# Adding the five weighed branches of a gated mix on VectorE instead of on TensorE

## The reference

```python
gate_in = jnp.concatenate([hidden_states, _stats(short), _stats(long_), _stats(wide), _stats(delta_out), _stats(v)], -1)
hdn = jax.nn.gelu(gate_in @ g1_w.T + g1_b, approximate=False)
logits = (hdn @ g2_w.T + g2_b).reshape(b, Ll, H, 5)
p = jax.nn.softmax(logits, -1)
o = w_ctx[..., 0:1] * short + w_ctx[..., 1:2] * long_ + w_ctx[..., 2:3] * wide + w_ctx[..., 3:4] * delta_out + w_val * v
o = o * jax.lax.rsqrt(jnp.mean(o * o, -1, keepdims=True) + 1e-05) * onorm_w
return o.reshape(b, Ll, HID) @ o_w.T
```

## Time and profile before

| what | value |
|---|---|
| time, median of 3 runs | 745.3 us (739.52 to 745.67) |
| the profiled execution | 743.56 us, of which the span is 741.8 us |
| busy over the span | PE 83%, PEld 60%, DVE 59%, ACT 38%, POOL 15% |
| stage 3 | about 350 to 480 us |

### The profile page before, as it was taken

How to read it: one execution, slowest core, us unless ns; L and a number is a source line. 1 busy time by engine, 2 the same in 40 slices (tenths; PEclk the granted TensorE clock), 3 DMA queues, 4 the chain that set the end, 5 groups by cost and what they waited for, 6 DMA issues and landing times. The chain is left out here.

```text
span 741.8 us, 17132 instructions
## 1 busy us (share of the span) xinstructions
PE 619.3 (83%) x7532; PEld 443.7 (60%) x7544; DVE 440.9 (59%) x878; ACT 283.9 (38%) x518; POOL 111.5 (15%) x93
## 2 busy tenths in 40 slices
PE   4668879999998999686999957499999784998984
PEld 2365466777767777675344545377787672655643
DVE  2942567848766785748176764203358593667764
ACT  2665534433443443214343532123232325554431
POOL 0001340250061025000101221162100010000000
PEclk9968999999999999978899997589999987999988
DMA  6500520330151031003200106030000000000001
GB/s 173 188 2 3 175 83 4 117 114 4 31 166 38 4 115 59 4 3 92 81 0 1 57 29 246 3 111 1 1 0 1 0 1 0 1 1 29 29 0 58
DMA packets 26537, 37.52 MB, mean 51 GB/s; under 512 B 4641, under 2 KB 13602, under 8 KB 26463
## 3 DMA queue, kind: packets, MB, share of 16 engines
q1 hardware_dynamic: 26463, 36.42, 15.2%
HBM read 34.31 MB, written 2.10 MB: 49 GB/s over the span
## 5 line engine op out<-in xcount | busy, mean ns | idle before, releaser
L295 DVE SCALAR_TENSOR_TENSOR arena<-bank,conv_w,arena 128x511 f32<-128x511 f32 (+2 forms) x72 | 53.1, 746 | 30.3 <-ACT arena L1056 14.7
L1428 POOL COPY arena<-v_win 128x256 f32<-128x256 f32 x32 | 21.1, 688 | 194.8 <-PE bank L718 194.7
L2071 ACT COPY arena<-bank 128x512 f32<-128x512 f32 x40 | 23.5, 586 | 63.4 <-PE bank L1956 38.5
L1956 PE MATMUL bank<-v_win,arena 128*128 128x256 f32 x192 | 45.7, 386 | 0.0
L2420 PE MATMUL bank<-v_win,arena 128*128 128x256 bf16 x288 | 36.5, 279 | 7.9 <-DVE arena L2507 6.9
L718 PE MATMUL bank<-arena 128*32 128x128 f32 x512 | 35.7, 409 | 8.2 <-ACT arena L1067 7.0
L1112 ACT COPY arena<-bank 128x512 f32<-128x512 f32 x40 | 21.6, 589 | 51.6 <-PE bank L840 51.6
L1956 PEld LDWEIGHTS bank<-v_win,arena 128*128 128x128 f32 x192 | 35.3, 190 | 8.6 <-issue 4.4
L1072 ACT COPY arena<-bank 128x256 f32<-128x256 f32 x32 | 19.3, 604 | 54.0 <-PE bank L731 54.0
L2410 PE MATMUL bank<-arena,v_win 128*128 128x512 bf16 x134 | 36.2, 400 | 3.7 <-DVE arena L2478 3.2
L2420 PEld LDWEIGHTS bank<-v_win,arena 128*128 128x128 bf16 x288 | 28.4, 100 | 16.6 <-DVE arena L2507 7.9
(11 more groups left out here) (274 smaller groups left out, 1389.8 us busy)
## 6 DMA issues: line engine op xcount, KB each, us to landing
arena<-in_toep_w SPq DMA_DIRECT2D x32, 256.0 KB, 2.9
arena<-in_toep_l SPq DMA_DIRECT2D x32, 256.0 KB, 3.6
arena<-in_xT SPq DMA_DIRECT2D x12, 512.0 KB, 4.7
arena<-in_x SPq DMA_DIRECT2D x4, 512.0 KB, 4.9
arena<-in_ctx SPq DMA_DIRECT2D x4, 512.0 KB, 3.9
out<-arena SPq DMA_DIRECT2D x4, 512.0 KB, 2.9
qkv_w<-in_qkv_wT SPq DMA_DIRECT2D x1, 768.0 KB, 5.3
v_win<-in_w_gateT SPq DMA_DIRECT2D x1, 768.0 KB, 6.7
```

The source lines that it names most:

```text
L295: return nc.vector.scalar_tensor_tensor(out=acc[:, j:L], in0=src[:, 0:L - j], scalar=conv_w[:, m, CONV_K - 1 - j:CONV_K - j], in1=acc[:, j:L],
L1956: i = mm(oo, src[:, k, f * P:(f + 1) * P], w[:, k, :], start=(k == 0), stop=(k == KT - 1 and f > 0))
L2071: nc.scalar.copy(dst(i), bank[n % RING].rearrange("p (t c) -> p t c", c=dst(i).shape[-1]))\
```

## The change

VectorE makes the whole sum. `weigh_rest(b)` has three more additions behind its old last one: `ps` plus `pwl` into `pd` over all 1024 columns, and then `pv` onto `pd` in two halves of 512 columns. The first waits for its direct predecessor in the queue, and the first half for the first. `mix_squares` and `head_norm` read `pd` in VectorE's memory (the view `o_half`) instead of banks 6 and 7. The twelve identity products of a batch go, with their waits, and on TensorE `statistics(b+2)` now comes between `logits(b+1)` and `turn_logits(b+1)`. No DMA is changed.

```diff
-                def mix(b, t):
-                    if t == 0:
-                        pe.wait_ge(s3["p_wl"].sem, s3["p_wl"].at(b, 3))
-                        pe.wait_ge(s3["p_v"].sem, s3["p_v"].at(b, 1))
-                        pe.wait_ge(s3["p_sd"].sem, s3["p_sd"].at(b, 3))
...
-                    mm(o, ident[:], A3[b % 2]["pv"][:, t, :], start=True, stop=False)
-                    mm(o, ident[:], A3[b % 2]["ps"][:, t, :], start=False, stop=False)
-                    i = mm(o, ident[:], A3[b % 2]["pwl"][:, 0, t, :], start=False, stop=True)
...
                     if b < B - 1:
                         logits(b + 1)
-                    mix(b, 0)
+                    if b < B - 2:
+                        statistics(b + 2)
                     if b < B - 1:
                         turn_logits(b + 1)
-                    mix(b, 1)
-                    if b < B - 2:
-                        statistics(b + 2)
-                    mix(b, 2)
-                    mix(b, 3)
...
-                        act.wait_ge(s3["mix_mm"].sem, s3["mix_mm"].at(b, i2 + 1))
-                        a(A3[b % 2]["sq_b"][:, i2 * 2 * D:(i2 + 1) * 2 * D], mix_bank(i2)[:], ACT.Square)\
+                        act.wait_ge(s3["o_sum"].sem, s3["o_sum"].at(b, i2 + 2))
+                        a(A3[b % 2]["sq_b"][:, i2 * 2 * D:(i2 + 1) * 2 * D], o_half(b, i2), ACT.Square)\
...
                     v.tensor_tensor(A3[u]["ps"], A3[u]["ps"], A3[u]["pd"], ALU.add).then_inc(s3["p_sd"].sem, 1)
+                    dve.wait_ge(s3["p_wl"].sem, s3["p_wl"].at(b, 3))
+                    dve.wait_ge(s3["p_sd"].sem, s3["p_sd"].at(b, 3))
+                    v.tensor_tensor(A3[u]["pd"], A3[u]["ps"], A3[u]["pwl"][:, 0, :, :], ALU.add).then_inc(s3["o_sum"].sem, 1)
+                    dve.wait_ge(s3["p_v"].sem, s3["p_v"].at(b, 1))
+                    dve.wait_ge(s3["o_sum"].sem, s3["o_sum"].at(b, 1))
+                    for i2 in range(2):
+                        t = slice(2 * i2, 2 * i2 + 2)
+                        v.tensor_tensor(A3[u]["pd"][:, t, :], A3[u]["pd"][:, t, :], A3[u]["pv"][:, t, :], ALU.add)\
+                            .then_inc(s3["o_sum"].sem, 1)
...
-                                        mix_bank(i2)[:].rearrange("p (g c) -> p g c", c=DK),
+                                        o_half(b, i2).rearrange("p (g c) -> p g c", c=DK),
```

More of the change, by code:

```diff
@@ L576, in layer @@
             "last_root": 0, "st_turned": 1, "st_out": 1, "hdn_mm": 4, "gelu": 4, "lg_mm": 1, "lg_rows": 1, "lg_rows_out": 1,
-            "lg_pre": 4, "lg_exp": 1, "lg_post": 5, "p_wl": 3, "p_v": 1, "p_sd": 3, "mix_mm": 2, "mix_sq": 2, "mix_ss": 4,
+            "lg_pre": 4, "lg_exp": 1, "lg_post": 5, "p_wl": 3, "p_v": 1, "p_sd": 3, "o_sum": 3, "mix_sq": 2, "mix_ss": 4,
             "r_head": 2, "o_turned": 2, "o_norm": 2, "oT_out": 2, "y_mm": 2, "res": 2, "ln_st": 9, "ln_rs": 1, "nm_out": 1,
@@ L1488, in layer, with o_half @@
         ST_BANK, LG_BANK = 0, 4
-        hid_bank, mix_bank, turn3_bank, y_bank = (lambda m: bank[2 + m % 2]), (lambda i2: bank[6 + i2]), (lambda k: bank[(1, 5)[k]]), (lambda i2: bank[i2])
+        def o_half(b, i2):
+            return A3[b % 2]["pd"][:, 2 * i2:2 * i2 + 2, :].rearrange("p t c -> p (t c)")
+        hid_bank, turn3_bank, y_bank = (lambda m: bank[2 + m % 2]), (lambda k: bank[(1, 5)[k]]), (lambda i2: bank[i2])
         with nc.Block() as block:
@@ L1553, in turn_logits @@
                     nc.tensor.transpose(bank[LG_BANK][:, P:2 * P], A3[b % 2]["lgr"], ident[:]).then_inc(s3["lg_mm"].sem, 1)
-                def mix(b, t):
-                    if t == 0:
-                        pe.wait_ge(s3["p_wl"].sem, s3["p_wl"].at(b, 3))
-                        pe.wait_ge(s3["p_v"].sem, s3["p_v"].at(b, 1))
-                        pe.wait_ge(s3["p_sd"].sem, s3["p_sd"].at(b, 3))
-                        if b:
-                            pe.wait_ge(s3["o_norm"].sem, s3["o_norm"].at(b - 1, 2))
-                    o = mix_bank(t // 2)[:, (t % 2) * D:(t % 2 + 1) * D]
-                    mm(o, ident[:], A3[b % 2]["pv"][:, t, :], start=True, stop=False)
-                    mm(o, ident[:], A3[b % 2]["ps"][:, t, :], start=False, stop=False)
-                    i = mm(o, ident[:], A3[b % 2]["pwl"][:, 0, t, :], start=False, stop=True)
-                    if t % 2:
-                        i.then_inc(s3["mix_mm"].sem, 1)
                 def turn_o(b):
```

## The result

The changed kernel takes 756.8 us (median of 4 runs, 752.69 to 758.24) against 743.94 us (median of 4, 739.52 to 745.67) for the kernel before: 1.0173 times as long, 95% interval 1.0109 to 1.0237. It is slower, the profiled execution by 14.5 us (758.09 against 743.56). Whoever reads only the medians learns little of the change, since the stages ahead of stage 3 bring up to 15 us of their own: in the thirteen profiles of this document stage 3 starts between 342.6 and 358.0 us, with the same work ahead of it. The trace divides the sum.

The account below looks back on a forecast made before the run. VectorE and TensorE were taken as balanced to 0.25 us in rounds 0 and 1. Profiled 743.6 plus 5.4 for the queues plus 5.8 for TensorE's clock gave 754.8 us, range 748.5 to 759.5.

Parts of the forecast that it names:

- The balance of 0.25 us: Rounds 0 and 1: VectorE would release turn_o only 0.25 us before TensorE is ready, so relieving TensorE gives back only that.
- a = 2.60: VectorE's weigh_rest: the three new additions lengthen it by 2.60 us a batch, with bounds 2.4 and 2.7.
- +3.04 and +2.35 by the queues: Delay from VectorE's additions without clock effects: +3.04 us in round 0, +2.35 in round 1, +5.4 in all.
- The clock, 2.9 a round: TensorE's turn_o and project in rounds 0 and 1 run at low clock after idling: 2.9 us each, 5.8 for two.
- the plain case: Both projections of rounds 0 and 1 at low clock, no slow hidden: 5.4 + 5.8 = 11.2 us, giving 754.8.
- Rounds 2 and 3 at nothing: weigh_rest(3)'s 2.60 us more stays under VectorE's 3.29 us idleness before residual(2), with 0.7 to spare: 0 added.
- The port at nothing: head_norm reading two SBUF operands beside GpSimd's power adds nothing; the lockout rival gave 756.6, chance 0.04.
- A clock that stays up (749.0): Rival: TensorE's clock stays full in rounds 0 and 1, leaving only 743.6 + 5.4 = 749.0 us; chance 0.09.
- TensorE as the pace (733.2): Rival: TensorE sets the pace and loses 5.2 us in each of two rounds, 733.2 us; chance of faster 0.05.
- No effect (743.6): Rival: the additions lie in unseen waits of VectorE and count in no round, 743.6 us; chance 0.04.
- The allowance of 1.7 for the median: Part of the range's upper end: 1.7 us because the median of runs lay above the profiled run.
- the two rows of the prediction, 2.22 and 3.10 us: TensorE idle stretches in the old profile: 2.22 us left the clock at 1.00; in one of 3.10 it fell.

Follow-up runs that it names:

- The queue order alone: Kernel before with TensorE's statistics and turn_logits put ahead of all twelve identity products, the sum staying on TensorE: stage 3 131.4 us, ratio 0.9974.
- spare products: Changed kernel with unread identity products in TensorE's idle stretches of rounds 0, 1: ratio 1.0104; kernel before with them in rounds 2, 3: 0.994, then 0.9928.
- the run without additions: Changed kernel without its three VectorE additions, the sum left out: stage 3 134.9 us, ratio 1.0054 to the kernel before.
- the halfway kernel: Kernel before with one more full VectorE addition, eight identity products a batch, changed TensorE queue order, unread products in rounds 2 and 3: 741.65 us, ratio 0.9948.

## Why the prediction was right

The forecast was 754.8 us, the range 748.5 to 759.5, slower by over 1% at 0.71. The measured 756.8 is 2.0 above it, and the mechanism is the one that was named: VectorE becomes the later engine in rounds 0 and 1, and TensorE's clock falls in the pauses. Stage 3 alone became 10.5 us longer against a sum of 11.2, but three errors are in that: the queues cost 0.6 more than the sum, rounds 2 and 3 cost 0.4 more (within their spread), and the clock 1.6 less. That they nearly cancel is luck.

- **The balance of 0.25 us.** Held. The queue order alone moved stage 3 by 0.4 and its first stretch by -0.4, and the additions put beside the old sum reproduced the whole loss.
- **a = 2.60.** Measured 390.10 - 386.24 = 3.86 from L1763 to the next step, less the old 1.14: 2.72 a batch, just above the upper bound of 2.7. The dependent steps start 0.10 after their predecessor's end (386.24 + 1.22 = 387.46, then 387.56), where I took 0.04 from instructions of 80 columns.
- **+3.04 and +2.35 by the queues.** With the clock kept up, 60.0 - 56.4 = 3.6 and 26.7 - 24.3 = 2.4. The queue sum was 5.4 and is 6.0: a counts three times in it, 0.36, and the 0.2 that is left stands ahead of the mix, in code that is the same (`logits(1)` starts 31.3 us after the stage's start with spare products and 31.0 in the kernel before).
- **The clock, 2.9 a round.** Overestimated: 2.6 and 1.5, 4.2 in place of 5.8. The term that was mis-sized is `hidden` behind its own pause, which I left out of the plain case and gave at most 1.5. In round 0 the clock had fallen in the pause before `hidden(2)`'s third product (391.98, 0.50 until 398). From there to the end `hidden(2)` took 13.2 us in place of 10.0, so the gap ahead of `turn_o(0)` was 3.25 and not 6.3. In round 1 `hidden(3)` began later than I had it (the wait for its input) and took 13.5 in place of 11.8, behind a pause of 4.15. The late start is not what closed the gap: with the load put earlier, the pause moved to the third product, and the end of `hidden(3)` stayed. The gap ahead of `turn_o(1)` was 1.57 and not 4.4, `turn_o(1)` ran at full clock with 1.09, and the clock fell only behind it, inside the pause for ScalarE: half the price, 5.25 for `project(1)` in place of 6.1. Of the signs that I had named, "idle for 4 to 6 us" ahead of both and 29.6 us between the second halves of `residual(0)` and `residual(1)` (28.2) did not come; the others did.
- **Rounds 2 and 3 at nothing.** Held to 0.4 us. The cover of `weigh_rest(3)` was 0.7 by the sum and 0.56 by the trace, and it is gone as soon as `project(2)` is warm.
- **The port at nothing.** Held for `head_norm` beside a power: 0.69 in rounds 0, 1 and 3 (in round 2 no power is beside it). That the trace does not agree with the page was too wide a reading of it. The Trainium skill ("SBUF — State Buffer", "SBUF: two separate sides") says that such instructions of the two engines lock each other out for a whole instruction. With additions of 1024 columns on GpSimd the trace agrees (3.37 in place of 1.22); with powers of eight columns it does not.
- **The rivals.** A clock that stays up (749.0) was made by hand with spare products, and then costs 6.0 in rounds 0 and 1 (138.2 in stage 3, with 1.2 more in rounds 2 and 3). TensorE as the pace (733.2) fell with the run without additions, which is not faster even with a = 0. No effect (743.6) fell with the additions put beside the old sum, which cost 10.5.
- **Outside the sum.** Of the profiled 14.5 us, 3.9 came from ahead of stage 3. The allowance of 1.7 for the median stood for such things, and the runs of the kernel before spread by 6 us themselves. With the 10.5 measured in stage 3 the sum would have been 743.6 + 10.5 = 754.1, and the rest up to 756.8 comes from elsewhere. How near the total is to the forecast says little, then; the stretches of stage 3 are the better test.

## What to carry to other kernels

Where two engines end within a fraction of a microsecond of each other, as here, work moved from one to the other was lost in full, but for what filled an old wait, and gained nothing; read both hand-over times in the trace before you move it. An engine that idles more may also be slower for it: TensorE's new idle stretches cost 4.2 us here through its granted clock, whether its own work had been taken away or not, and products that nobody reads, put into stretches in which it idled anyway, made even the old kernel 0.7% faster (1.4% was measured with a few more at the stage's ends, of which those at its start showed in the trace).

## What the runs showed of the hardware

- A 128x1024 float32 addition on GpSimd and an instruction of VectorE with both operands in SBUF hold each other up: 3.37 us for VectorE in place of 1.22, 2.82 in place of 0.69, 2.00 in place of 0.24 for one of 80 columns, and 3.26 for GpSimd in place of 2.33. A power of 128x8 columns on GpSimd (1.6 us) did nothing of the sort.
- An idle stretch of only 1.57 us, with a second of 0.92 close behind it, was followed by the low clock (439.8 in the changed kernel), while the work between them, eight transposes, ran at full clock. The length of a pause alone does not tell: in the halfway kernel one of 1.36 us with 0.92 behind it left `project(0)` at full clock (3.72), and one of 1.71 with 0.92 behind it was followed by the low clock (5.26 for `project(1)`). The same pause of 1.00 us in the same code was followed by 1.00 in one execution and by 0.56 in another. So the two rows of the prediction, 2.22 and 3.10 us, were too few to tell which pause ends low.
- A dependent 128x1024 instruction on VectorE starts 0.10 us after its predecessor's end; an independent one 0.08 before it.
